# A graph layer's chain of running maxima: final rows from three stretches, steps placed for the finals too, final additions on one engine

## What is computed

```python
h = jnp.maximum(_layernorm(x, axis=-1), 0.0)
x_i, x_j = h[dst], h[src]
msg = jnp.concatenate([x_i, x_j - x_i], axis=-1) @ W.T + b
out = jax.ops.segment_max(msg, dst, num_segments=6250)
return x + jnp.where(jnp.isfinite(out), out, 0.0)
```

## Time and profile before

| | us |
|---|---|
| Median of 3 runs | 991.62 (990.52 to 994.15) |
| The profiled execution, its own time | 995.42 |
| Its span, first to last instruction | 993.8 |
| PE busy, PE weight loads busy | 564.1, 265.1 |
| DVE busy | 846.5 |
| ACT busy | 577.9 |
| POOL busy | 713.8 |
| Mean granted TensorE clock | 0.825 of full |

### The profile page before, as it was taken

The page is one execution under the profiler, slowest core; times in us unless marked ns, Lnnn a source line. Parts: engine busy times, 40 slices in busy tenths (PEclk is TensorE's granted clock), DMA queues, the critical chain, the costliest instruction groups (busy, mean ns, idle before and its releaser), DMA issues.

```text
span 993.8 us, 7917 instructions
## 1 busy us (share of the span) xinstructions
PE 564.1 (57%) x2393; PEld 265.1 (27%) x2393; DVE 846.5 (85%) x1237; ACT 577.9 (58%) x255; POOL 713.8 (72%) x644
## 2 busy tenths in 40 slices
PE   2556970000002366766776676788878888676560
PEld 2443640000001122322222232333333333222240
DVE  7899899987785598999989999899999999758573
ACT  3775113000038999597996987496797976844000
POOL 1587878888875677677767676676777677777745
PEclk9898995555555779888878987999999999988875
DMA  8831222212146466656657776998988778754344
GB/s 256 194 97 21 70 71 79 67 50 77 55 145 217 142 208 223 197 174 222 179 170 232 255 253 201 295 296 300 338 302 321 278 239 259 227 186 139 73 79 148
DMA packets 62901, 182.11 MB, mean 183 GB/s; under 512 B 20358, under 2 KB 33140, under 8 KB 56315
## 3 DMA queue, kind: packets, MB, share of 16 engines
q1 hardware_dynamic: 42530, 140.13, 40.7%
q0 software_dynamic: 20144, 40.52, 17.1%
q10 hardware_dynamic: 184, 0.96, 0.3%
HBM read 127.34 MB, written 55.04 MB: 184 GB/s over the span
## 4 chain that ended last, share of the span: by engine, by line
POOL 29%; DVE 26%; issue 19%; DMA 13%; PE 8%; ACT 3%; POOLq 0%; DVEq 0%; SPq 0%; PEldq 0%
POOL rows L669 22%; DVE acc L1191 10%; DMA rows<-near_table,idx 8%; PE ps L787 8%; DVE maxima L1134 5%; POOL ohs L641 4%; POOL hT L648 3%; DVE hT L1141 3%; DMA running_max<-maxima 2%; DVE pos L878 2%; DVE hT L1154 1%; DVE ohs L1179 1%; DMA ohs<-in_dst,begin_i 1%; DMA ohs<-winners 1%; DVE hT L1146 1%
## 5 line engine op out<-in xcount | busy, mean ns | idle before, releaser
L669 POOL DMA_INDIRECT rows<-near_table,idx x527 | 600.3, 1139 | 206.0 <-issue 138.8
L787 PE MATMUL ps<-ohs,near 128*128 128x481 bf16 x1443 | 351.9, 401 | 142.6 <-DVE acc L1191 119.7
L1191 DVE TENSOR_TENSOR acc<-ps,acc 128x1924 f32<-128x1924 f32 x192 | 336.5, 1779 | 21.8 <-PE ps L787 21.6
L1134 DVE SCALAR_TENSOR_TENSOR maxima<-maxima,fresh,rows 128x128 f32<-128x128 f32 x527 | 185.6, 352 | 72.6 <-DMA rows<-near_table,idx 56.2
L787 PEld LDWEIGHTS ps<-ohs,near 128*128 128x128 bf16 x1443 | 143.7, 105 | 350.1 <-DVE acc L1191 125.8
L548 ACT ACTIVATE ohs<-ohs,neg_l 128x6272 bf16<-128x6272 bf16 x25 | 137.9, 5518 | 123.4 <-DMA ohs<-winners 123.4
L541 ACT ACTIVATE hT<-k,off 128x2400 bf16<-128x2400 int16 x49 | 108.9, 2281 | 131.7 <-DVE hT L1146 115.6
L550 ACT ACTIVATE ohs<-ohs 128x6272 bf16<-128x6272 bf16 x25 | 135.8, 5431 | 0.8
L787 PE MATMUL ps<-sorts_mem,near 128*128 128x481 bf16 x468 | 107.8, 385 | 32.7 <-DVE acc L1191 28.6
L773 PE MATMUL ps<-flags,ones 128*128 128x8 f32 x2 | 0.6, 356 | 173.0 <-DVE spare L1167 173.0
L641 POOL DMA_INDIRECT ohs<-src_pad,start_i x49 | 55.0, 1122 | 34.9 <-DVE start_i L891 20.5
(11 more groups left out here) (173 smaller groups left out, 517.4 us busy)
## 6 DMA issues: line engine op xcount, KB each, us to landing
ohs<-winners SPq DMA_DIRECT2D x37, 1568.0 KB, 7.7
running_max<-maxima SPq DMA_DIRECT2D x90, 512.0 KB, 5.1
sorts_mem<-winners SPq DMA_DIRECT2D x12, 1568.0 KB, 8.0
rows<-near_table,idx POOLq DMA_INDIRECT x527
acc<-in_x SPq DMA_DIRECT2D x6, 512.0 KB, 8.2
near_table<-acc SPq DMA_DIRECT2D x12, 256.0 KB, 4.5
base<-in_x SPq DMA_DIRECT2D x1, 2744.0 KB
out_x<-hT SPq DMA_DIRECT2D x12, 224.0 KB
```

Of the source, the lines that this page charges most:

```text
L669: nc.gpsimd.indirect_dma_start(rows[:, n % (SLOTS * GATHERS), :], None, near_table[:, :], bass.IndirectOffsetOnAxis(idx[:, n:n + 1], 0)).t ...
L787: last = nc.tensor.matmul(bank(4 * (n % 2) + c - UNITS[r][0])[:, 0:CHUNK], near[:, t, part, :], oh[t % OHS][:, at:at + CHUNK], start=part ...
L1134: V.scalar_tensor_tensor(run_at(n + 1), run_at(n), fresh[:, n:n + 1], rows[:, n % (SLOTS * GATHERS), :], ALU.add, ALU.max).then_inc(chain, 1)
L1191: V.tensor_tensor(into, found, into, ALU.max).then_inc(max_done, 1)
```

## The change

`CUT` becomes a table `HOMES` of three stretches (first and last column, first step, step limit), so there are three tables: columns 0 to 35 with steps up to 415, columns 36 to 43 with steps 232 to 503, columns 44 to 48 with steps from 296 on. The nine early groups stay where they were. Groups 9 and 10 now wait for the stores up to step 503 only, groups 11 and 12 for the last. Steps 296 to 415 are stored three times; in all 27 stores are added to 90. Two flags and a few small instructions are added for the end rows.

In `schedule()` a gather costs 1.45 us before the words pieces, 2.0 from there to the first round, 1.28 after, each fourth tile's third round costs 3.65 (the one-hot that DVE makes), and POOL's clock counts the early groups of finals. All additions of `base` are on DVE, right behind each join.

```diff
-CUT, CUT_CAP, CUT_LOW = 36, 416, 232
+HOMES = ((0, 36, 0, 416), (36, 44, 232, 504), (44, 49, 296, 528))
+EARLY = HOMES[0][1] // GROUP
...
-        pieces += [("round", 1.85)] * 4
+        pieces += [("round", 1.85)] * 2 + [("round", 3.65 if t % 4 == 0 else 1.85)] + [("round", 1.85)]
...
+    phase, gather = "lists", {"lists": 1.45, "words": 2.0, "round": 1.28}
+    ending = [FINALS_FROM + g * FINALS_EVERY for g in range(EARLY)]
...
+        if name in gather:
+            phase = name
...
-                issue += GATHERS * (1.3 if name == "round" else 1.85)
+                issue += GATHERS * gather[phase]
                 landed += [issue + 3.0] * GATHERS
+                if n + GATHERS in ending:
+                    issue += GATHERS * gather[phase]
...
-    kept = (CUT_CAP, STEPS + CT - CUT_LOW)
+    kept = [cap - low + STEPS * (low > 0) for _, _, low, cap in HOMES]
...
-            return [(0, n)] * (n < CUT_CAP) + [(1, 0)] * (n == 0) + [(1, n - CUT_LOW + STEPS)] * (n >= CUT_LOW)
+            return [(h, n - low + STEPS * (low > 0) if n else 0) for h, (_, _, low, cap) in enumerate(HOMES)
+                    if n == 0 or low <= n < cap]
...
-                if by_pool(g):
-                    sp.wait_ge(final_added, g // 2 + 1)
-                else:
-                    sp.wait_ge(final_ready, g + 1 - min(g // 2 + 1, groups // 2))
+                sp.wait_ge(final_ready, g + 1)
...
-            stored(all_blocks)
-            for g in range(early_groups, groups):
+            for g in range(EARLY, groups):
+                for home in HOMES[1:]:
+                    if spans[g][0] == home[0]:
+                        stored(home[3] // STEPS)
                 finals(g)
-            for g, (a, z) in enumerate(spans):
-                if by_pool(g):
-                    pool.wait_ge(joined, g + 1)
-                    nc.gpsimd.tensor_tensor(rowsF[:, a:z, :], rowsF[:, a:z, :], base[:, a:z, :], ALU.add).then_inc(final_added, 1)
...
-                if not by_pool(g):
-                    dve.wait_ge(joined, g + 1)
-                    V.tensor_tensor(rowsF[:, a:z, :], rowsF[:, a:z, :], base[:, a:z, :], ALU.add).then_inc(final_ready, 1)
+                dve.wait_ge(joined, g + 1)
+                V.tensor_tensor(rowsF[:, a:z, :], rowsF[:, a:z, :], base[:, a:z, :], ALU.add).then_inc(final_ready, 1)
```

More of the change, by code:

```diff
@@ L344, in by_dve @@
             return t % 4 == 3
-        def by_pool(g):
-            return g % 2 == 0 and g < groups - 1
         def act_count(t):
@@ L646, in finals @@
                 for j in range(a, z):
-                    h = 0 if j < CUT else 1
+                    h = sum(j >= end for _, end, _, _ in HOMES)
                     nc.gpsimd.indirect_dma_start(
@@ L675, in _ @@
                             pool.wait_ge(m_ready, len(batches))
-                            stored(CUT_CAP // STEPS)
+                            stored(HOMES[0][3] // STEPS)
                         finals(g)
@@ L681, in _ @@
                 pool.wait_ge(max_done, rounds * tiles)
-                for g in range(early_groups):
+                for g in range(EARLY):
                     pool.wait_ge(final_in[g], 16 * GROUP)
@@ L1048, in loser_words @@
                 if h:
[L1049 to L1054 removed]
+                    for i, (begin, end, low, most_steps) in enumerate(HOMES):
+                        of = slice(max(begin, a), end)
+                        if end < z:
+                            then(V.tensor_scalar(flags[:, 6 + i:7 + i], tot[:, end - a:end - a + 1],
+                                                 float(most_steps - first - 1), None, ALU.is_gt))
+                        if low:
+                            then(V.tensor_scalar(flags[0:lastp, 7 + i:8 + i],
+                                                 tot[0:lastp, begin - a:begin - a + 1], float(low - first), None, ALU.is_lt))
+                        then(V.tensor_scalar(end_f[:, of], tot[:, of.start - a + 1:end - a + 1], float(first),
+                                             float(most_steps - 1), ALU.add, ALU.min))
                     settled()
[L1056 removed]
+                    for begin, end, low, _ in HOMES[1:]:
+                        then(V.tensor_scalar(end_f[:, begin:end], end_f[:, begin:end], float(STEPS - low), 0.0, ALU.add, ALU.max))
                 else:
@@ L1064, in loser_words @@
                 settled()
-                for at, end, rows_kept in ((a, CUT, kept[0]), (CUT, z, kept[1])) if h else ((a, z, kept[0]),):
+                for at, end, rows_kept in ([(max(u[0], a), u[1], r) for u, r in zip(HOMES, kept)] if h else [(a, z, kept[0])]):
                     then(V.scalar_tensor_tensor(end_row[:, at:end], part_f[:, 0:1].to_broadcast([P, end - at]),
```

18 lines of the change are left out of this document (5 added, 13 removed).

## The result

The changed kernel takes 998.17 us (median of 20 runs, 991.43 to 1005.01), the kernel before 993.44 beside it (20 runs, 989.41 to 996.29). The ratio is 1.0057, with a 95% interval of 1.0035 to 1.0079: it is slower by about half a per cent. The profiled execution has a span of 998.9 us and took 1000.5; against the 993.8 of the old one that is +5.1 us, which is the sum to be explained. (In some later sessions the kernel before itself took 1088 to 1101 us, and what ran there is read by its ratio alone, in experiment 10; ratios, unlike medians, leave out single executions more than 1.5% above the fastest.)

The account below looks back on a forecast made before the run. DVE was taken to carry the middle of the kernel and POOL's gathers the end. The last dense round's end moves +8.5 us and the part behind it -19.8, so 991.6 - 11.3 = 980.3 us, range 964 to 999.

Parts of the forecast that it names:

- Behind T: From the end of the last dense round (T) to the program's end: 20.9 us instead of 40.7, -19.8.
- The start of the rounds: Ahead of round 0: more chain steps before the second tree delay it and the first round, +12 us.
- Waits that go and come: DVE's gather waits: 29 us from 845 to 953 go, 22 us come from round 0 on.
- three signs of being wrong: Gather waits from the first round above 38 us, first load not moving, or final rows landing after the last round.
- waits that come: In the rounds: steps placed earlier than POOL's gathers land make DVE wait, +22 us.
- small terms: Minor items: four steps moved ahead of the last round's end +1.5, PE +2, end-row instructions 0, 27 more stores 0 or a few us.
- my upper bound: In the rounds: most DVE would wait if loads expose landings and half is regained, 45 us in all.
- "+2" for PE: In the last ten rounds, which have no steps: DVE waits for PE's matmuls, 0 to 3.5 us, taken as +2.
- The sum: Shift of the last dense round's end: 12 - 29 + 22 + 1.5 (four steps) + 2 = +8.5 us.
- the third: Rival: POOL's total sets the pace, waits only move from end to middle, 991 us; chance 0.20.
- the second: Rival: in the rounds, loads delay rows used right behind landing, DVE stops, PE's clock falls, 1003 us; chance 0.18.
- The first rival: In the tree stage, gathers are not held up by DVE; waits that come about 7 us, 965 us; chance 0.05.

Follow-up runs that it names:

- experiment 10: Eight more runs of changed-kernel variants with other gather prices or round costs, in sessions where the kernel before took 1088 to 1101 us; ratios such as 0.9873 and 0.994.
- experiment 4: Changed kernel with gather prices raised from 1.45 to 1.85 and 2.0 to 2.3 us, so fewer steps precede the second tree: 968.66 us, ratio 0.9729.
- experiment 2: Kernel before with the new schedule() and nothing else, two stretches and GpSimd's additions kept: 1008.87 us, ratio 1.0132.
- experiment 1: Changed kernel (three stretches, all additions on DVE) with the old schedule(), so only the tail is new: 980.96 us, ratio 0.9864.

## Why the prediction was wrong

I said 980.3 us and 0.62 for faster. The changed kernel took 998.17, 18 us above that; it is inside the range (964 to 999), but slower than the kernel before, for which I had 0.18. In terms of the profiled spans: -11.3 forecast, +5.1 measured. Most of the parts came out; two terms failed, the waits that come in the rounds (stores among them) and the wait for PE.

- **Behind T: right.** -19.8 forecast (20.9 us left), -20.6 measured (20.1 left). The timeline shows 0.69 + 0.69 and some handing over per group, no GpSimd addition, and the chain's last step at 957.5, 21 us ahead of T.
- **The start of the rounds: right, slightly high.** +12 forecast, +9.8 measured; the second tree ended at 302.5 where I had worked out 302.6. What I had not seen is that this term is the cheapest to undo: experiment 4 wins 25.6 us at tile 0, two and a half times the term.
- **Waits that go and come, for gathers alone: near.** -29 + 22 forecast; 29.0 went and 18.0 came, -11.0. All three signs of being wrong that I had named look at gathers, the first load and the final rows, and none of them showed: the fault lay in a wait that none of them watches.
- **The step that failed: "waits that come", +22, as a wait for gathers alone, with stores under the small terms ("27 more 512 KB stores ... 0, or a few us").** The wait for stores grew from 2.2 to 17.8 us, +15.6. The reason given (a step meets its store only eight steps later) overlooked that eight steps are two thirds of a tile at 12 steps a tile, and that the stores of those eight stand behind a table load. The timeline of the changed kernel:

```profile
541.90 0.33 SPq L416 DMA_DIRECT2D ohs<-winners  x1
...
543.08 12.64 SPq L421 DMA_DIRECT2D running_max<-maxima  x4
...
550.17 1.12 DVE L1137 SCALAR_TENSOR_TENSOR maxima<-maxima,fresh,rows 128x128 f32<-128x128 f32 x3
...
554.54 0.35 DVE L1137 SCALAR_TENSOR_TENSOR maxima<-maxima,fresh,rows 128x128 f32<-128x128 f32 x1 [3.26 <-DMA running_max<-maxima]
```

The load is issued at 541.90. Behind it the half is stored twice, since two stretches overlap there: the row groups four stores, the first two of which were issued at 543.08 and 543.45 and landed at 552.30 and 554.45. So of the batch at 550.17 three steps run, and the fourth, the first to write that half again, starts only at 554.54, after 3.26 us of waiting. It isn't a price of the 27 stores, though: with the same order and without them the two waits together are 37.3 us for 35.8 (experiment 2), and under the old order the 27 raise the store waits by 4.9 only (experiment 1). So it belongs to the sum of the waits that come. I had worked out how much slower POOL is than DVE, and counted as waits only what was left of the lead; what the steps needed was slack for rows and stores both. With gathers and stores together 35.8 us came, where I had 22 and my upper bound was 45.
- **The second step that failed: "+2" for PE.** DVE's wait for PE grew by 9.2 us, not 2. I looked at the last ten rounds alone. The timeline shows these as I had them, some 2 us a tile without a step:

```profile
956.39 1.16 DVE L1137 SCALAR_TENSOR_TENSOR maxima<-maxima,fresh,rows 128x128 f32<-128x128 f32 x3
...
961.93 3.73 DVE L1194 TENSOR_TENSOR acc<-ps,acc 128x1924 f32<-128x1924 f32 x2 [1.24 <-PE ps L784]
...
971.00 2.16 DVE L1194 TENSOR_TENSOR acc<-ps,acc 128x1924 f32<-128x1924 f32 x1 [1.29 <-PE ps L784]
```

But the new order spreads the steps unevenly long before: in tiles 25 to 48, 23 of 24 tiles had exactly 8 steps before, with 0.21 us of PE wait each, and 6.3 in all; with the change 12 of these tiles have 0 to 4 steps and wait 0.98 us each for PE, the 10 with 8 steps wait 0.52, and all 24 wait 18.2. My reading is that in a tile with few steps DVE gets ahead of PE and gives the time back. It is read from the two traces, by counting steps by tile; no run tested it alone, and the growth in the tiles with 8 steps is not explained by their own steps. A lower clock doesn't explain it: the mean granted clock over these tiles is 0.94 before and 0.97 with the change. Tail only (18.8) and the runs with the new order (23 to 36) agree with the reading.
- **The sum:** 12 - 7 + 1.5 + 2 = 8.5 was forecast for T. Stores (+15.6) and PE (+7.2 more) raise it, the start (-2.2) and gathers (-4.0) lower it, the steps and the rest add 0.6: 25.7.
- **The rivals.** The outcome lies between the third (the gain is eaten, 991) and the second (no slack behind the loads, 1003, from waits above 38). The second named the mechanism: rows used right behind their landing, a lower granted clock in the stage with the waits (0.92 for 0.99), waits of 35.8 us near its point of decision. The clock is a weak sign of it, though: the tree stage is at 0.86 before with hardly a gather wait, and at 0.84 now. I held against this rival that a wait gives the lead back; as I read it, it does so only for the steps at hand, since the order places the next ones as early again. The first rival is gone: gathers still take longer beside the tree's first minimum (that at 546.78 took 1.40 us, one in a free stretch 0.94). The Trainium skill (SBUF — State Buffer, Who interferes with whom) infers that a tensor_tensor does not hold up the writing of descriptors. The prediction set that against the row too flatly: the same section says that a DVE instruction with two SBUF inputs contends with a GpSimd instruction that reads SBUF, and this gather reads its offsets from `idx` there. The 2.19 us of the earlier trace rows and the 1.40 here agree with that second rule; no run separates the two, or any other cause of the pause.
- Right were also the first load (304.3 for "near 303") and the shift of gather waits out of the stage behind 845 (1.6 us). The growth of the wait for ACT was 5.4 us, not 9.

## What to carry to other kernels

An order that places work as early as a cost table allows has two prices, and the table's small constants set both: work placed ahead of the item that starts a pipeline delays the whole pipeline (here 20 steps ahead of the second tree, 7 us of work, were worth 26 us at tile 0, and moving 12 of these behind that tree alone, with the same number ahead of the first round, 16 us), and work placed right behind its data turns every slow landing into a stall. When a wait is removed, ask which semaphore would come last next: store, gather and PE waits took each other's place in these runs, so sum DVE's waits over all releasers between two fixed events before pricing one of them. Split a change into its parts early: the tail of this one was worth 13 us, and its order lost more than that.

## What was unexpected of the hardware

How long a transfer takes to land goes with how long ago a table load (1,568 KB) was issued. In the trace of the changed kernel, by issue and landing of each of the 117 stores of 512 KB: 9.3 us on average for the 25 issued within 3 us of the last load, 4.2 for the 26 issued 5 to 8 us after it, and 3.3 for the 22 issued 14 us or more after it. A batch of four gathers landed a median of 6.2 us after the last of them ended when that was within 3 us of a load (22 batches, 3.3 to 8.1), and 1.6 when it was 11 us or more after it (23 batches, 1.5 to 7.5). Halving the stores shortened this little: over all issues 256 KB took a median of 4.5 us and 512 KB 4.3; by the distance to the load it was 8.1 us on average for 9.3 within 3 us of it, and 2.4 for 3.3 from 14 us on.
